# A decoder layer on one core: weight loads issued by another engine, stores of x by ScalarE, routing matmuls in a bank of their own

## What is computed

```python
x = x + self_attention(layernorm(x))           # 16 heads, 4 kv heads, causal
x = x + cross_attention(layernorm(x), ctx)     # 16 heads, 64 context tokens per sequence
x = x + experts(layernorm(x))                  # 8 experts, each token goes to its top 2
# experts: sum over the two of weight * (silu(h @ w0[e]) * (h @ w1[e])) @ wo[e]
```

## Time and profile before

| | |
|---|---|
| median of 3 runs | 960.01 us (959.10 to 960.25) |
| profiled execution | 958.15 us, span 956.4 us |
| PE busy | 857.5 us, 90% of the span |
| DVE, ACT, POOL busy | 547.3, 446.9, 266.5 us |
| DMA | 76.89 MB, mean 80 GB/s |
| mean granted TensorE clock | 0.965 of full |

### The profile page before, as it was taken

The page is one execution under the profiler, slowest core; times in us unless marked ns, Lnnn a source line. Parts: engine busy times, 40 slices in busy tenths (PEclk is TensorE's granted clock), DMA queues, the critical chain, the costliest instruction groups (busy, mean ns, idle before and its releaser), DMA issues.

```text
span 956.4 us, 15581 instructions
## 1 busy us (share of the span) xinstructions
PE 857.5 (90%) x5165; PEld 737.8 (77%) x5166; DVE 547.3 (57%) x1579; ACT 446.9 (47%) x1130; POOL 266.5 (28%) x392
## 2 busy tenths in 40 slices
PE   5999999999999999997888979696953999999995
PEld 4788889998899888996666858675842877888884
DVE  5777666665666666564776758766746722232321
ACT  3666656665666656664524434252442622223231
POOL 1233222332233222332020201602452322323232
PEclk9999999999999999999998989998975999999998
DMA  8001997000000000000392434627884232333232
GB/s 307 1 1 38 293 300 194 1 1 2 1 1 1 23 1 1 1 2 1 114 174 48 74 78 89 155 38 228 190 293 156 32 52 45 51 49 54 47 54 28
DMA packets 64449, 76.89 MB, mean 80 GB/s; under 512 B 3328, under 2 KB 56704, under 8 KB 64256
## 3 DMA queue, kind: packets, MB, share of 16 engines
q1 hardware_dynamic: 48656, 54.12, 23.0%
q0 software_dynamic: 7152, 9.34, 6.1%
q10 hardware_dynamic: 8576, 12.58, 3.9%
HBM read 30.65 MB, written 28.61 MB: 62 GB/s over the span
## 4 chain that ended last, share of the span: by engine, by line
PE 33%; DMA 7%; DVE 4%; SPq 3%; ACTq 2%; ACT 2%; issue 1%; POOLq 0%; DVEq 0%
PE bank_y L1684 7%; SPq L898 3%; PE bank_s L40 2%; DMA b_VW_lo<-b_VWs_lo 2%; PE bank_s L41 2%; PE bank_s L42 2%; DMA out_dram<-x_all 2%; PE bank_s L1534 2%; PE bank_o L1675 2%; DMA out_dram<-b_y,b_rows 1%; PE bank_y L40 1%; PE bank_q L40 1%; PE bank_y L42 1%; PE bank_y L41 1%; PE bank_t L40 1%
## 5 line engine op out<-in xcount | busy, mean ns | idle before, releaser
L271 POOL TENSOR_TENSOR a_prob<-a_prob,a_rinv 128x128 f32<-128x128 f32 (+1 forms) x256 | 124.6, 508 | 307.1 <-DVE a_rinv L363 304.9
L334 DVE TENSOR_TENSOR a_pT_lo<-bank_t,a_pT_hi 128x384 fp32r<-128x384 f32 x128 | 70.6, 552 | 99.2 <-ACT a_pT_hi L286 99.2
L286 ACT ACTIVATE a_pT_hi<-bank_t 128x384 fp32r<-128x384 f32 x128 | 62.8, 491 | 115.3 <-PE bank_t L476 115.3
L297 ACT ACTIVATE a_prob<-a_masked,a_negmax 128x128 f32<-128x128 f32 (+1 forms) x256 | 114.0, 454 | 0.0
L1042 POOL DMA_INDIRECT out_dram<-b_y,b_rows x39 | 62.8, 1609 | 160.0 <-DVE b_y L1466 157.0
L396 DVE CUSTOM_DVE_ANT_0 a_masked<-bank_s,a_causal 128x128 f32<-128x128 f32 (+1 forms) x256 | 80.3, 351 | 9.2 <-PE bank_s L42 9.2
L1459 DVE TENSOR_TENSOR b_xT_lo<-bank_o,b_xT_hi 128x256 fp32r<-128x256 f32 x39 | 16.6, 425 | 118.4 <-ACT b_xT_hi L1176 118.4
L40 PE MATMUL bank_s<-a_kT_hi,a_qT_hi 128*128 128x128 f32 (+1 forms) x256 | 80.7, 315 | 0.0
L1684 PE MATMUL bank_y<-b_We,b_interT 128*128 x312 | 75.3, 384 | 2.1 <-issue 1.3
L40 PE MATMUL bank_y<-a_WprojT_hi,a_oT_hi 128*128 128x256 f32 x256 | 72.6, 284 | 3.2 <-DVE a_oT_lo L334 3.2
L1022 POOL TENSOR_TENSOR b_prob<-b_prob,b_rinv 128x1024 f32<-128x1024 f32 x16 | 30.5, 1906 | 151.4 <-DVE b_rinv L1250 151.4
(11 more groups left out here) (360 smaller groups left out, 2405.5 us busy)
## 6 DMA issues: line engine op xcount, KB each, us to landing
slots<-a_nobody SPq DMA_DIRECT2D x1, 16641.0 KB, 67.4
b_VW_hi<-b_VWs_hi SPq DMA_DIRECT2D x16, 512.0 KB, 7.1
b_VW_lo<-b_VWs_lo SPq DMA_DIRECT2D x16, 512.0 KB, 9.9
b_W<-in_L_ffn_w_kernel_dram ACTq DMA_DIRECT2D x16, 512.0 KB, 6.9
b_rows<-slots SPq DMA_DIRECT2D x39, 129.0 KB, 2.1
b_We<-in_L_ffn_wo_kernel_dram ACTq DMA_DIRECT2D x8, 512.0 KB, 9.8
a_stage<-n_L_attn_weight_qkv_dram SPq DMA_DIRECT2D x5, 512.0 KB, 8.2
x_WqT<-in_L_xattn_Wq_dram SPq DMA_DIRECT2D x1, 2048.0 KB, 8.4
```

The lines of the kernel that those rows point to most:

```text
L271: pool.tensor_tensor(prob[:, u % 3, a:b], prob[:, u % 3, a:b], rinv[:, u % 4, i:i + 1].to_broadcast([P, b - a]), ALU.mult)\
L286: act.activation(dst.hi, src, ACT.Copy).then_inc(half[n], 1)
L297: act.activation(prob[:, u % 3, a:b], masked[:, u % 2, a:b], ACT.Exp, scale=-1.0, bias=negmax[:, u % 4, i:i + 1], accum_out=rowsum[:, u % ...
L334: dve.tensor_tensor(dst.lo, src, dst.hi.bitcast(F32), ALU.subtract).then_inc(free[n], 1)
```

## The change

The loads of expert weights go from ACT's program to SP's: W 0 and 1 between the two moves of pair 3 (once the `m` fills of that pair are copied), the first four `We` after the second move, W 2 and 3 when the moves have landed, 4 and 5 when the last scores have been read, 6 and 7 after the last output. The stores of x go from SP to ACT, to the head of `pack` for groups 0 to 3 and into (4, 1) for group 4. `gate` and `rank` always use bank y1. `split_hi` of W 0 and 1 goes from (3, 2) to (4, 0), and that of 2 and 3 to behind the last slot. The fills of the third slots keep their order.

```diff
     def use_fill(name, banks, i):
-        order.use(banks[i % len(banks)], name, READER.get(name[0], "both"))
+        n = "y1" if name[0] in ("gate", "rank") else banks[i % len(banks)]
+        order.use(n, name, READER.get(name[0], "both"))
@@ SyncE
                     move(p, b)
-                if p > 0:
-                    store_x(p - 1)
-            for g in (GL - 1, GL):
-                store_x(g)
+                    if (p, b) == (PAIRS - 1, 0):
+                        for i in range(NM):
+                            at = ("m", p, i)
+                            sp.wait_ge(free[order.bank(at)], order.free(at))
+                        for e in (0, 1):
+                            load_w(e)
+            for e in range(4):
+                load_we(e)
+            for moved in VW_moved:
+                sp.wait_ge(moved, 64 * PAIRS)
+            for e in (2, 3):
+                load_w(e)
+            sp.wait_ge(shifted, 2 * NT)
+            for e in (4, 5):
+                load_w(e)
+                load_we(e)
+            sp.wait_ge(y_done, NT)
+            for e in (6, 7):
+                load_w(e)
+                load_we(e)
@@ ScalarE
+            def store_x(g):
+                first, n = GROUPS[g]
+                act.wait_ge(y_added, first + n)
+                if g > 0:
+                    act.wait_ge(x_stored, 16 * g)
+                act.dma_start(out[first * P:(first + n) * P, :].rearrange("(t p) k -> p t k", p=P),
+                              x_all[:, first:first + n, :]).then_inc(x_stored, 16)
+
             def pack(g):
                 first, n = GROUPS[g]
+                store_x(g)
...
-                if (p, t) == (PAIRS - 1, 0):
-                    for e in (0, 1):
-                        load_w(e)
-                    for e in range(4):
-                        load_we(e)
-                if (p, t) == (PAIRS - 1, 3):
-                    for e in (4, 5):
-                        load_w(e)
-                        load_we(e)
                 if (p, t) == (PAIRS, 1):
                     exp_gap(GL - 1)
-                    act.wait_ge(y_done, NT)
-                    for e in (6, 7):
-                        load_w(e)
-                        load_we(e)
+                    store_x(GL)
                     pack_again(GL)
...
-                if (p, t) == (PAIRS - 1, 2):
-                    for moved in VW_moved:
-                        act.wait_ge(moved, 64 * PAIRS)
-                    for e in (2, 3):
-                        load_w(e)
+                if (p, t) == (PAIRS, 0):
                     split_hi(0, 1)
-                if (p, t) == (PAIRS, 0):
-                    split_hi(2, 3)
             exp_gap(GL)
-            split_hi(4, 5)
+            split_hi(2, 3, 4, 5)
```

More of the change, by code:

```diff
@@ L900, in move, with load_w, load_we @@
                             .then_inc(VW_moved[b], 16)
[L902 to L908, removed]
+            def load_w(e):
+                for half_of, w in enumerate((w0, w1)):
+                    sp.dma_start(W.lo[:, 2 * e + half_of, :].bitcast(F32).rearrange("p (c n) -> p c n", c=HC),
+                                  w[e].rearrange("(c p) n -> p c n", p=P)).then_inc(w_loaded[e], 16)
+            def load_we(e):
+                sp.dma_start(We[:, e, :, :], we[e].rearrange("(c p) n -> p c n", p=P)).then_inc(we_loaded, 16)
             for p in range(PAIRS):
@@ L1089, in exp_gap @@
                 act.activation(gap[:, 0:n], gap[:, 0:n], ACT.Exp).then_inc(gap_exp, 1)
[L1091 to L1098, removed]
             def split_hi(*of):
```

## The result

The changed kernel takes 948.28 us (median of 4 runs, 945.78 to 952.55), the kernel before 959.99 beside it. The ratio is 0.9898, 95% interval 0.9872 to 0.9923: 1.0% faster, 9.8 us. The forecast was 21 us and a median of 939.0; the measured one lies at the edge of the range of 932 to 949. The profiled execution, the fastest of the four, took 945.78 us (span 944.0), 12.4 us less than that of before. It is a lucky one, and says so itself: 2.3 us of its gain arise in slot (0, 2), where nothing was changed.

What follows compares the result with a forecast made beforehand. PE bounds the experts, unaltered by the change; the worth must come from PE's holes in cross attention. Terms 5.0 + 3.2 - 0.7 + 13.5 = 21.0 us, taking the median from 960.01 to 939.0, range 932 to 949.

Steps and rivals of the forecast that it cites:

- the sum for pair 3: Slots (3, 0) to (3, 3): earlier exponentials and low halves, less the scatter wait, plus clock; 13.5 us gained.
- The third slots of pairs 1 and 2: Cross attention: stores on ACT gain 5.0 us in pair 2, 3.2 in pair 1; `gate` in y1 costs 0.7.
- Slot (3, 0): Weight-load issue gone from ACT and `rank` in y1: PE and DVE go on, next exponential 8.9 us earlier.
- What is late next: DVE's `weigh_again` then waits for four scatters; 1.5 us of the 8.9 given back (0 to 4.5).
- so the middle is right: Scatters landing between 669.0 (quiet DMA) and 674.5 (beside moves), second moves starting about 664: 671.5 taken.
- Slot (3, 3): Exponential and copy no longer behind weight-load issue: low halves 5.2 us earlier, plus 0.9 for PE's clock.
- Stores: Third slots: x stores on ACT, `vw` copy then waits for moves, matmuls at full clock; 5.0 us pair 2, 3.2 pair 1.
- Gate in y1: Third slots of pairs 1 and 2: `gate` waits for bank y1; 0.7 us each, half taken, together -0.7.
- Moved onto SP: Weight loads on SP arrive in time under slots (3, 0) to (4, 1), late `split_hi` hidden; cost 0.
- rival (d): Slower: SP's one queue delays weights, second expert tile stalls 20 us; median 962, chance 0.05.
- if the moves land later than 12 us: Sign of being wrong, for moves on SP's queue: landing takes over 12 us.
- Rival (a): DMA takes it back: `weigh_again` 3 us later, stores gain less, POOL loses 2; gain 11, median 949, chance 0.20.

Runs made afterwards that it cites:

- e5: The changed kernel itself, unaltered, run again on another chip: 950.17 us against 960.91 for the kernel before, ratio 0.9897.
- e4: The changed kernel with `gate` and `rank` back in the bank rotation: 944.48 us, ratio to the kernel before 0.9855.
- e1: The kernel before with only `gate` and `rank` always in bank y1: 958.82 us against 957.40, ratio 1.0027.
- e12: The changed kernel with pair 3's second moves waiting for group 1's first four scatters, `gate` still in y1: 944.89 us, ratio to the kernel before 0.9855.
- e14: The changed kernel with `gate` rotating and pair 3's second moves waiting for group 1's first four scatters, repeated: 940.93 us, ratio to the kernel before 0.9827.
- e9: The changed kernel with `gate` rotating and pair 3's second moves waiting for group 1's first four scatters: 938.92 us against 958.89, ratio 0.9807.
- e2: The kernel before with only the stores of x issued by ACT: 953.37 us, ratio to the kernel before 0.9953.
- e3: The changed kernel with the stores of x back on SP: 951.45 us, ratio to the kernel before 0.9943.
- e8: The changed kernel with `gate` back in the rotation, only `rank` fixed in y1: 947.48 us, ratio to the kernel before 0.9858.
- e13: The changed kernel with only `gate` back in the rotation, repeated on another chip: 947.04 us, ratio to the kernel before 0.9865.

## Why the prediction was right or wrong

The gain is 9.8 us where 21.0 were forecast. The step that failed is the sum for pair 3: 13.5 us were forecast, 6.2 are there in the profiled execution and 3.9 in e5. Its first term was right, its price for what is late next was set too low, and its term for slot (3, 3) too high. The third slots of pairs 1 and 2 were forecast at 7.5 us with `gate`'s loss; from the exponential of t = 2 to that of t = 3 they are 4.6 us shorter together (5.2 in e5).

**Slot (3, 0), forecast 8.9 us: right.** 8.3 us in the first step. Without the issue PE and DVE run through. That the issue alone would give 4.6 us was right too: e4 has the loads on SP and the banks as before, and its first step is 4.8 us shorter than that of the kernel before. The bank alone, e1, makes it 3.5 shorter; the two add.

**What is late next, forecast 1.5 us given back: mis-sized.** The mechanism and the place are those of the text, the scatter wait in `weigh_again`, but 4.2 us are given back, at the slow end of "0 to 4.5". The starts were forecast well. Set back by the 7.4 us that were won ahead of (3, 0), the first scatter is issued at 661.9 (forecast 661.1), the last at 665.8 (665.0), and the moves begin at 663.6 ("at about 664"). What fails is the sentence "so the middle is right": DVE waits for the last scatter, and that one is issued after the moves, so that the slow landing of 9.5 us of the prediction's own rows applies to it and not a mean with 4.0. It landed after 8.9 us. "The scatter wait is in front of scores that PE has done already" is true, but doesn't make the wait cheap: PE had nothing else, idled 3.59 us and ran at half pace after. The landings are 2.8 to 3.5 us in e4, where the moves start behind the scatters, and 9 beside the moves of another queue. The Trainium skill ("DMA: Bandwidth & Descriptors", section "Queues, rings and completion order") states that each DMA engine takes turns between the queues it has work for, packet by packet. The trace agrees in so far as the scatters slow down beside another queue's moves; the turns themselves no view shows.

**Slot (3, 3), forecast 5.2 us and 0.9 for the clock: mis-sized, the largest part of the miss.** The third and fourth steps together give 2.1 us where 6.1 were forecast. The exponential's own delay went (its 2.8 us), and ACT's copy follows at 683.93. But the scores reached DVE late, for the slow clock behind the hole. From the exponential of (3, 2) to DVE's low halves, the forecast's own mark, it is 17.4 us before and 16.2 changed: 1.2 won where 5.2 were forecast. With the collision gone it is 13.8 in e12 and 13.0 in e14, 3.6 and 4.4 won, so this term was nearly right for a kernel without the collision. It isn't kept to the end: the third and fourth steps of e12 and e14 together are only 0.7 and 1.9 us shorter than before, in part since the last scatters then land late beside the weight loads. What of this is POOL's chain of scatters, which the forecast did name, no run parts.

**Pair 3 in all:** forecast 13.5. From the exponential of (3, 0) to the first row load it is 74.3 us before and 68.1 changed, 6.2 won; with the moves waiting and `gate` rotating it is 63.9 in e14 and 66.1 in e9, so 10.4 and 8.2 won. The profiled gain of 12.4 us is made up of 7.4 us ahead of (3, 0) (2.3 of them before the exponential of (0, 3)), these 6.2, and 1.3 lost in the experts.

**Stores, forecast 5.0 and 3.2 us: the mechanism right, the sum too large.** The moves release the `vw` copy, as forecast, at 616.50 (620.5 in the times of before, since the work ahead is 4.05 us earlier; the forecast was 619.6). The third slot of pair 2 is 3.4 us shorter and that of pair 1 1.2, `gate`'s loss included. The 1.9 us for the clock came in full in neither: in pair 2 the four matmuls behind the hole take 2.53 us, and in pair 1 they are at full pace but the scores of (1, 3) then fall to half pace. In e5 the two are 3.6 and 1.6. e2 and e3 measure both stores together at 4.5 and 4.3 us.

**Gate in y1, forecast -0.7: mis-sized.** The hole is there, 0.56 and 0.55 us, and the whole of it counts, with 0.3 of latency, in each slot, 1.7 in all. The profiles bear this out: the two third slots take 40.5 us together in the mean of the five that have the stores on ACT and `gate` in y1, and 38.8 in the mean of the eight that have `gate` rotating. e8 and e13 put the price at 3 to 4 us; what is above 1.7 no row shows, and in e8 it is at least in part luck.

**Moved onto SP, forecast 0: right for the weights.** No expert tile waits for them, and rival (d) is out: the loads stand in SP's queue and the first rows come at 716.71 (forecast near 709). One of the prediction's signs of being wrong did appear, "if the moves land later than 12 us": the last of the second moves landed after 13.1 us, at 673.0, harmless here, as PE reads it at 687.56. Another is the clock, which still drops about the third slots. The rule that the prediction cites from the Trainium skill ("DMA: Bandwidth & Descriptors", section "Issuing engines are not separate DMA queues") counts saved issue time as small beside the transfer; here the time saved is what e4's first step shows, 4.8 us, since the issue stood ahead of a copy that PE and DVE were waiting for.

**Rival (a)** describes the outcome, with its 949, and most of its path: `weigh_again` comes 3.1 us later than the forecast took it (the rival said 3), and the stores gave 4.3 to 4.5 us, nearer to its 3.2 than to the 8.2 of the forecast. What it lacks is the slow clock behind PE's hole. I gave it 0.20 and the forecast 0.66.

Open stays why identical executions of the changed kernel spread over 6.8 us (945.78 to 952.55) where the kernel before showed 1.2 beside it, though 7.9 in the 19 runs beside e1. The profiles differ in how many holes of 2 to 4 us are followed by slow matmuls, in places that the change doesn't touch as well, such as (0, 2).

## What to carry to other kernels

When a stall is removed, list every DMA that its end released: these are brought forward too, and the price of the change is what they meet, here scatters that took 3 us alone and 9 beside them. A transfer with slack (here the moves, landed by 673.0 and read at 687.56) should be made to wait for one that someone is about to need; one wait on SP gave back 4 us that the change had lost. Then list what stands behind the waiting transfer: in e14 the next scatters came earlier by it, and met the weight loads. An idle time on an engine that is "done already" isn't free on TensorE, if the next matmuls then run at half pace. And before a microsecond of one profile is put down to a change, look at a stretch that the change doesn't touch: here such a stretch alone varied by 3.1 us.

## What the runs showed of the hardware

Issuing a 512 KB store on ACT's queue took 0.44 us in pair 1 and 0.38 in pair 2 of the changed kernel, while SP's own issues beside it took 2.1 and 3.1 us: the backlog belonged to SP's queue and not to both. Four scatters with no move beside them landed in 2.8 to 3.5 us (e4), beside four moves of 512 KB in 9 us, and beside weight loads in some 6 (e14). Holes of 3.7 us in one place (0, 2) were followed by matmuls at half pace in one execution (3.78 us for four) and at full pace in another (1.98 us). The prediction counts slow matmuls behind holes of over 5 us; they also stand behind one of 3.64 us in the kernel before (0, 2) and one of 1.87 in the changed kernel.
